# Diffusion steps on Trainium2: who turns the finished sums back into rows

## The chip, the cores and the metric

The kernel runs on one core of one Trainium2 chip. The metric is the device time of one launch in microseconds. The kernel before was run three times: 2592.35, 2608.69 and 2619.11 us, with a median of 2608.69 us.

## The reference, cut to what matters

Four graph layers follow one another on 3125 nodes with 128 features and 50000 edges. Only the last, a diffusion, is touched. With `norm` made of the nodes' degrees (a self loop counts one) and `t_norm` the softmax of `t` over its ten rows, it computes:

```python
def step(h, _):
    h = jax.ops.segment_sum(norm[:, None] * h[row], col, num_segments=N)
    return (h, h)
_, hs = jax.lax.scan(step, x, None, length=STEP - 1)
y = t_norm[0] * x + jnp.einsum('kf,knf->nf', t_norm[1:], hs)
```

Then `y` goes through a weight matrix, bias and ReLU, and is added to the layer's input. All values are 32-bit floats.

## The kernel before, in words

The nine sparse sums are done as dense matrix products. The kernel keeps `counts`, a 3200 by 3200 matrix in 16 bits that says how often each source node sends to each target node. It is cut into 25 blocks of 128 source nodes (`NB`). By Horner's rule a step computes sums over sources of (rows of `y`) times (row of counts) and adds `t_norm[k] * x`; there are nine steps (`STEPS - 1`).

**Matmuls.** In a step each source block `sb` is the stationary operand, 128 nodes by 128 features. So the product comes out turned: features lie on partitions, target nodes on columns. A source is split into a high and a low part in rounded 32-bit form (`U_parts`, `u_part(sb, 0)` and `u_part(sb, 1)`), and both are multiplied and added in PSUM. The last source, 24, has both parts in one block of partitions. Target nodes are cut into four ranges (`RANGES`): three of 896 columns and one of 448. In the first three ranges odd and even columns are separate matmuls of 448 columns. The odd counts are read from `counts` in place as 32-bit words; the even counts have to be converted first into a tile of the ring `T_even` (`TILES` tiles of 448 columns). The fourth range is converted whole. One source in one range is a *piece*: four matmuls in the first three ranges, two in the fourth, half of it for source 24.

**Order.** `visits()` writes the order out. In the middle of a step one source goes through all four ranges (the pieces are `paired`). At a step's ends it is range by range: the first `LAG` sources at the beginning, the last `LAG` at the end. So range 0 is complete before the other ranges, and the next step can begin on its first blocks. Pieces are numbered through all steps, `FULL` = 100 in one step. `range_end` has the place in the step at which each range is complete.

**What goes beside the matmuls.** ScalarE and VectorE each run through all piece numbers n in one loop, and each issues at place n what its tables put there. Both are strictly in order, and a wait holds all that stands behind it.
- Even counts of piece n + `AHEAD`. In paired pieces ScalarE converts ranges 0 and 1 with one instruction (line 2921), VectorE 2 and 3 (line 2997). In unpaired ones they take turns (`by_act`, lines 2924 and 2997). A conversion waits until the piece that used its tile is done.
- `summed(s, r)` (VectorE, lines 2967, 2970 and 2971): once the last piece of a range is done, PSUM plus `t_norm[k]` times the turned input `x` is written to SBUF, in `W[r % 2]`. The turned input has been brought there by a DMA of SyncE's queue from `turned_rows`; for range r the queue waits until the range that last used the same half of `W` has been turned.
- `turn(s, t)` (TensorE, line 2843): up to four blocks of a finished range are transposed against the identity into a PSUM bank. `TURNS` lists seven such groups, with range, first block, blocks and bank; `places` says at which piece numbers they come. In each group TensorE waits for `d_summed`.
- `high(s, t)` (ScalarE, line 2882) and `low(s, t)` (VectorE, line 2956) read the turned blocks from PSUM, scale them by the nodes' degrees and write the high part and the rest as `U_parts` of the next step.

In the last step nothing is turned; `products` multiplies the sums by the weights directly. In the first step sources come in the order `SOURCES`, as their counts return from DRAM, and `turn_h` and `kept` also turn the layer's input for `turned_rows`.

A first matmul of a range in a step waits for `d_summed` (its bank has been read) and, where a bank was also used for turning (`freed`), for `d_split` (its low parts have been made).

Of the kernel before, what the change touches and what calls it, by code (L numbers as in the profile page):

```python
# [13 lines left out]
P = 128  # L14
D = 128
N = 3125
NB = -(-N // P)
# [114 lines left out]
def build(nc, a, out):  # L132
    ctx = ExitStack()
    with ctx:
# [2119 lines left out]
        RANGES = [(0, 2 * HALFW), (2 * HALFW, 2 * HALFW), (4 * HALFW, 2 * HALFW), (6 * HALFW, HALFW)]  # L2254
        TILES = 8
        tiles_at = -(-(tables_at + 32) // P) * P - 32
        turned_at = tiles_at + TILES * HALFW
        U_at = turned_at + 2 * 2 * HALFW
        UW = (NB - 1) * 2 * D + D
# [381 lines left out]

        LAG = 6
        END = NB - LAG

# [11 lines left out]
        def diffusion(begin, ends):  # L2656
# [6 lines left out]
            COUNT = len(PIECE)  # L2663
            AHEAD = 5
            assert COUNT == FULL * (STEPS - 1)
            paired = [len(ranges) == 4 for s, sb, ranges in VISITS for r in ranges]
            by_act = lambda n: PIECE[n][2] < 2 if paired[n] else n % 2 == 0
            evens = [sum(by_act(m) == by_act(n) for m in range(n + 1)) for n in range(COUNT)]
# [5 lines left out]

            TURNS = [(0, 0, 4, 0), (0, 4, 3, 1), (1, 7, 4, 2), (1, 11, 3, 3), (2, 14, 4, 4), (2, 18, 3, 7), (3, 21, 4, 6)]
            NT = len(TURNS)
            places = [range_end[0] + 1, range_end[0] + 3, range_end[1] + 1, range_end[1] + 3, FULL + 1, FULL + 3, FULL + 5]
            turn_at = {FULL * s + place: (s, t) for s in range(STEPS - 2) for t, place in enumerate(places)}
            turns_of = [2, 4, 6, 7]
            freed = {0: 7, 1: 7, 2: 14, 3: 14, 4: 18, 6: NB}  # L2680

            last = STEPS - 2
            GROUPS = [(0, 0, 4, 7), (0, 4, 3, 0), (1, 7, 4, 1), (1, 11, 3, 2), (2, 14, 4, 3), (2, 18, 3, 4), (3, 21, 4, 5)]
            group_at = {FULL * last + place: g for g, place in enumerate((*places[0:4], range_end[2] + 2, range_end[2] + 4))}
            NGS = len(GROUPS)
# [8 lines left out]
            HS = [space.get([2 * P]) for _ in range(3)]  # L2694
            W = [at(turned_at + k * 2 * HALFW, [2 * HALFW]) for k in range(2)]
            space = Space(at, U_at, U_at + END * 2 * D)
            XR = space.get([NB, D])
# [31 lines left out]
            def turned_in(bank, q, n=P):  # L2729
                return banks[0:n, bank, q * P:(q + 1) * P]  # L2730

            def turns_made(s, r):

                return NT * s + turns_of[r]

# [55 lines left out]
            def pe(e):  # L2791
                def matmuls(v):
# [8 lines left out]
                    for j in range(parts):  # L2801
                        weight = U_parts[:, sb * 2 * D + j * D:sb * 2 * D + (j + 1) * D]
                        start, stop = sb == order[0] and j == 0, sb == order[-1] and j == parts - 1
                        for i, r in enumerate(ranges):
                            n = FIRST[v] + i
                            d0, w = RANGES[r]
                            if start and s:
                                e.wait_ge(d_summed, 4 * (s - 1) + r + 1)
                                if 2 * r in freed:
                                    e.wait_ge(d_split, NB * s + freed[2 * r])  # L2810
                            if r < 3:
                                w0 = sb * NP // 2 + d0 // 2
# [18 lines left out]

                def turn(s, t):
                    r, b0, n, bank = TURNS[t]
                    e.wait_ge(d_summed, 4 * s + r + 1)
                    if bank == 7 and s == 0:
                        e.wait_ge(h_copied.sem, h_copied.at(len(PAIRS)))
                    elif bank == 7:
                        e.wait_ge(d_split, NB * s + b0 + n)
                    for q in range(n):
                        b = b0 + q  # L2840
                        c0 = b * P - RANGES[r][0]
                        rows = P if b < LAST else HALF
                        x = e.transpose(turned_in(bank, q, rows), turned_sum(r)[:, c0:c0 + rows], ident)
                    x.then_inc(d_turned, 1)

                def products(g):
# [10 lines left out]
                for v, (s, sb, ranges) in enumerate(VISITS):  # L2857
                    matmuls(v)
                    n = FIRST[v] + len(ranges) - 1
                    if n in pair_at:  # L2860
                        turn_h(pair_at[n])
                    if n in turn_at:
                        turn(*turn_at[n])
                    if n in group_at:
# [3 lines left out]
            def act(e):  # L2868
# [6 lines left out]

                def high(s, t):
                    r, b0, n, bank = TURNS[t]
                    e.wait_ge(d_turned, NT * s + t + 1)
                    for q in range(n):
                        b = b0 + q  # L2880
                        rows = P if b < LAST else HALF
                        e.activation(u_part(b, 0, rows), turned_in(bank, q, rows), ACT.Copy, scale=rows_of(dinv2l, b, rows)[:, b:b + 1]).then_inc(d_hi, 1)

# [27 lines left out]
                for n in range(-8, COUNT):  # L2911
# [16 lines left out]
                    if n in pair_at:  # L2928
                        kept(pair_at[n])
                    if n in turn_at:  # L2930
                        high(*turn_at[n])
                    if n in group_at:
# [7 lines left out]
            def dve(e):  # L2940
# [7 lines left out]

                def low(s, t):
                    r, b0, n, bank = TURNS[t]  # L2950
                    e.wait_ge(d_turned, NT * s + t + 1)
                    e.wait_ge(d_hi, NB * (s + 1) + b0 + n)
                    for q in range(n):
                        b = b0 + q
                        rows = P if b < LAST else HALF
                        e.scalar_tensor_tensor(u_part(b, 1, rows), turned_in(bank, q, rows), rows_of(dinv2l, b, rows)[:, b:b + 1], u_high(b, rows),
                                               ALU.mult, ALU.subtract).then_inc(d_split, 1)
# [31 lines left out]
                for n in range(-8, COUNT):  # L2989
# [569 lines left out]
```

## Time and profile before

| what | before |
|---|---|
| median of 3 runs | 2608.69 us (2592.35 to 2619.11) |
| the profiled execution's own time (its span, first to last instruction) | 2609.8 us |
| TensorE matmul busy | 2312.7 us (89%), 12453 matmuls |
| VectorE busy | 1439.1 us (55%) |
| ScalarE busy | 1231.7 us (47%) |
| GpSimd busy | 1202.3 us (46%) |
| diffusion, first matmul to last sum of the fourth range | 1914.0 to 2598.6 us |

The profile is one execution of the program as the hardware profiler recorded it. The span reaches from its first instruction to its last. Busy times of an engine are sums over its instructions; instructions overlap a little, since the next one starts before the last has ended, so distances between starts say more about throughput than durations do. In the diffusion the matmul records carry modelled ends, and starts are the better guide there too. Times in the order-of-time views are microseconds from the span's start, and what stands in brackets behind a row is how long the engine was idle before it and what it waited for. Tiles are named as `out<-in`: what is written, then what is read.

### The profile page before, as it was taken

The numbers are of one execution on the slowest core, as the hardware profiler recorded it, in microseconds if no ns is written. First come the engines' busy times: TensorE is split into PE (matmuls) and PEld (weight loads), VectorE is DVE, ScalarE is ACT, GpSimd is POOL, SyncE is SP. The second block draws the span as 40 slices with busy tenths as digits, with TensorE's granted clock in tenths as the row PEclk, the third lists the DMA queues.
The fourth block names the chain that finished last, engine by engine and source line by source line (L and its number), as shares of the span: only waits on it lengthen the run. The fifth ranks groups of instructions, "written<-read, shape, count | busy, mean of one in ns | idle before, by whom it ended". The sixth has DMA issues, their size and how long they took to land.

```text
span 2609.8 us, 51354 instructions
## 1 busy us (share of the span) xinstructions
PE 2312.7 (89%) x12453; PEld 1966.3 (75%) x12453; DVE 1439.1 (55%) x6252; ACT 1231.7 (47%) x5343; POOL 1202.3 (46%) x1243
## 2 busy tenths in 40 slices
PE   3778777789539999999989999999989999999998
PEld 2556556555429999999947888888879889988887
DVE  5767777760535665666446777758543433344343
ACT  3656666667313333333233555546454444444443
POOL 3777777720057777777147777777330000000000
PEclk9955555569755555555589989979799999999999
DMA  3242333340334444444054344444452000000002
GB/s 92 60 124 65 123 94 90 122 121 2 91 102 105 108 109 110 110 108 134 21 135 111 105 113 114 113 105 117 139 219 78 29 11 22 18 25 25 25 25 62
DMA packets 174356, 227.43 MB, mean 87 GB/s; under 512 B 63552, under 2 KB 134409, under 8 KB 173929
## 3 DMA queue, kind: packets, MB, share of 16 engines
q0 software_dynamic: 50176, 131.74, 18.9%
q1 hardware_dynamic: 117070, 88.93, 11.2%
q10 hardware_dynamic: 6810, 3.40, 0.5%
q8 instruction: 111, 1.82, 0.3%
q14 instruction: 189, 1.54, 0.2%
HBM read 183.63 MB, written 40.29 MB: 86 GB/s over the span
## 4 chain that ended last, share of the span: by engine, by line
PE 70%; issue 9%; DVE 7%; POOL 5%; ACT 4%; DMA 3%; ACTq 1%; DVEq 0%; SPq 0%; POOLq 0%
PE banks L2817 9%; PE banks L2813 9%; PE banks L1780 6%; PE banks L1781 6%; PE banks L1722 5%; POOL arena L229 4%; PE banks L1783 4%; PE banks L1786 3%; PE banks L755 3%; PE banks L2819 3%; PE banks L967 2%; PE banks L2424 2%; PE banks L1784 2%; PE banks L758 2%; PE banks L782 1%
## 5 line engine op out<-in xcount | busy, mean ns | idle before, releaser
L229 POOL DMA_INDIRECT arena<-value_table,arena x392 | 391.4, 998 | 314.1 <-DMA ed_table<-arena 195.0
L229 POOL DMA_INDIRECT arena<-gat_table,arena x392 | 403.4, 1029 | 198.4 <-issue 86.8
L2813 PE MATMUL banks<-counts,u_parts 128*128 128x448 f32 x1323 | 490.9, 371 | 2.8 <-DVE u_parts L2946 2.8
L2817 PE MATMUL banks<-counts_even,u_parts 128*128 128x448 f32 x1323 | 485.9, 367 | 0.0
L229 POOL DMA_INDIRECT arena<-h_table,arena x392 | 377.5, 963 | 128.1 <-issue 87.8
L2997 DVE CAST counts_even<-counts 128x448 fp32r<-128x448 bf16 x450 | 162.7, 389 | 304.3 <-PE banks L2817 275.4
L755 PE MATMUL banks<-arena 128*128 128x425 bf16 x392 | 208.2, 531 | 112.6 <-ACT arena L811 93.8
L758 PEld LDWEIGHTS banks<-arena 128*128 128x128 f32 x784 | 230.9, 311 | 54.2 <-issue 43.1
L2813 PEld LDWEIGHTS banks<-counts,u_parts 128*128 128x128 f32 x1323 | 249.1, 188 | 23.9 <-ACT arena L2441 3.0
L2817 PEld LDWEIGHTS banks<-counts_even,u_parts 128*128 128x128 f32 x1323 | 249.2, 188 | 21.4 <-ACT counts_even L2921 0.3
L1781 PE MATMUL banks<-arena 128*128 128x17 f32 x784 | 230.6, 375 | 0.0
L1780 PE MATMUL banks<-arena 128*128 128x17 f32 x784 | 228.6, 373 | 0.1
L808 ACT ACTIVATE arena<-banks 128x400 f32 x392 | 207.9, 530 | 36.4 <-DVE banks L744 25.4
L1722 PE MATMUL banks<-arena 128*128 128x512 bf16 (+1 forms) x605 | 216.4, 412 | 3.9 <-DMA ed_table<-arena 3.9
L1871 ACT ACTIVATE arena<-banks 128x32 f32 (+1 forms) x784 | 187.5, 239 | 60.9 <-issue 38.8
L2921 ACT ACTIVATE counts_even<-counts 128x896 fp32r<-128x896 bf16 x123 | 117.4, 954 | 206.0 <-PE banks L2817 194.5
L1781 PEld LDWEIGHTS banks<-arena 128*128 128x128 f32 x784 | 214.2, 333 | 0.0
L1780 PEld LDWEIGHTS banks<-arena 128*128 128x128 f32 x784 | 201.8, 318 | 7.2 <-DVE arena L1653 0.4
L758 PE MATMUL banks<-arena 128*128 128x17 f32 x784 | 176.7, 307 | 12.9 <-DMA arena<-h_table,arena 12.2
L1783 PE MATMUL banks<-arena 128*128 128x136 f32 x784 | 186.3, 323 | 0.0
L1859 ACT ACTIVATE arena<-banks 128x2 f32<-128x2 f32 (+1 forms) x262 | 45.7, 175 | 293.6 <-PE banks L1786 208.0
L755 PEld LDWEIGHTS banks<-arena 128*128 128x128 bf16 x392 | 49.5, 126 | 153.5 <-ACT arena L811 142.3
(298 smaller groups left out, 4842.7 us busy)
## 6 DMA issues: line engine op xcount, KB each, us to landing
adj_rows<-arena SPq DMA_DIRECT2D x5, 4000.0 KB
arena<-ed_table SPq DMA_DIRECT2D x784, 0.5 KB
arena<-turned_rows SPq DMA_DIRECT2D x27, 448.0 KB, 3.3
counts<-adj_rows SPq DMA_DIRECT2D x1, 7200.0 KB, 20.3
arena<-h_table,arena POOLq DMA_INDIRECT x392
arena<-value_table,arena POOLq DMA_INDIRECT x392
arena<-gat_table,arena POOLq DMA_INDIRECT x392
counts<-adj_rows SPq DMA_DIRECT2D x1, 5600.0 KB, 17.6
```

Of the source, the lines that this page charges most:

```text
L229: return e.indirect_dma_start(into, None, table, bass.IndirectOffsetOnAxis(ap=index.bitcast(U32), axis=0))
L755: e.matmul(banks[:, c % RBANK, W1:CS], BY_LO[:, kx, :], BY_HI_D[:, kx, 0:CC], start=True, stop=True, skip_group_check=True)
L758: e.matmul(banks[:, c % RBANK, 0:W1], G[:, k, :], S[:, c // BC % 2, c % BC, :], start=False, stop=True, skip_group_check=True).then_inc(l0 ...
L808: e.activation(first.of(C, j), windows_in(j)[:, 1:, 0:WIN], ACT.Copy, scale=SMALL).then_inc(l0_counted, 1)
L1722: e.matmul(banks[:, 7, 0:n], identb, spare[:, 0:n], start=True, stop=True, skip_group_check=True)
L1780: e.matmul(pv[:, 0, :], rows[:, 0:D], OHF[k3][:, j, :], start=begins, stop=True, skip_group_check=True)
L1781: e.matmul(pv[:, 1, :], rows[:, D + H:], OHV[k3][:, j, :], start=False, stop=True, skip_group_check=True)
L1783: e.matmul(pv[:, 0:H, :], rows[:, 0:D], S[c % RS][:, 0:H, :], start=begins, stop=True, skip_group_check=True)
L1871: e.activation(first.of(acc, c), sums_in(c)[:, :, 0:WIN], ACT.Copy).then_inc(e2_acc, 1)
L2813: e.matmul(banks[:, 2 * r, 0:HALFW], weight, C_odd[:, w0:w0 + HALFW], start=start, stop=stop)
L2817: x = e.matmul(banks[:, 2 * r + 1, 0:HALFW], weight, tile(n), start=start, stop=stop)
L2997: e.tensor_copy(into, counts).then_inc(d_even_dve, 1)
```

## The change

VectorE turns the finished sums, not TensorE. `e.transpose` of VectorE turns 32 by 32 squares. One instruction takes the squares (i, j) of all blocks of a range: it reads partitions 32i to 32i + 31 and writes partitions 32j to 32j + 31 of `V`, a new SBUF region of seven blocks. Sixteen such instructions (`QUADS`) turn a range; in the last range block 24 has 64 nodes, and j of 2 and 3 leave it out. Two instructions are issued at each of eight places in a row. ScalarE's high parts and VectorE's low parts read `V` in SBUF instead of PSUM. `V` holds one range, so `turn` waits until high and low parts of the range before have been made; this follows from the order of the places.

The places are new: counted from one before range 0's end, the sums come at 3, 13, 27 and 33, the turns begin at 5, 19, 34 and 48, the high parts come at 13, 16, 27, 30, 42, 45 and 56, the low parts begin at 15, 29, 44 and 58. `LAG` goes from 6 to 7. The room for `V` comes from the ring of even counts: `TILES` goes from 8 to 6 and `AHEAD` from 5 to 4. In unpaired pieces ScalarE converts two of three, where it was one of two. The matmuls no longer wait for `freed` banks. One addition of weights moves from the third to the fourth step.

```diff
-        TILES = 8
+        TILES = 6
-        U_at = turned_at + 2 * 2 * HALFW
+        U_at = turned_at + 3 * 2 * HALFW
-        LAG = 6
+        LAG = 7
-            AHEAD = 5
+            AHEAD = 4
-            by_act = lambda n: PIECE[n][2] < 2 if paired[n] else n % 2 == 0
+            by_act = lambda n: PIECE[n][2] < 2 if paired[n] else n % 3 > 0
-            TURNS = [(0, 0, 4, 0), (0, 4, 3, 1), (1, 7, 4, 2), (1, 11, 3, 3), (2, 14, 4, 4), (2, 18, 3, 7), (3, 21, 4, 6)]
-            NT = len(TURNS)
-            places = [range_end[0] + 1, range_end[0] + 3, range_end[1] + 1, range_end[1] + 3, FULL + 1, FULL + 3, FULL + 5]
-            turn_at = {FULL * s + place: (s, t) for s in range(STEPS - 2) for t, place in enumerate(places)}
-            turns_of = [2, 4, 6, 7]
-            freed = {0: 7, 1: 7, 2: 14, 3: 14, 4: 18, 6: NB}
+            RANGE_BLOCKS = [(0, 7), (7, 7), (14, 7), (21, 4)]
+            QUADS = [(i, j) for j in range(4) for i in range(4)]
+            NQ = len(QUADS)
+            first_end = range_end[0] - 1
+            at_places = lambda rows: {FULL * s + first_end + p: (s, *v) for s in range(STEPS - 2) for p, v in rows}
+            sum_at = at_places([(3, (0,)), (13, (1,)), (27, (2,)), (33, (3,))])
+            sum_at.update({FULL * (STEPS - 2) + range_end[r] - 1: (STEPS - 2, r) for r in range(4)})
+            turn_at = at_places([(p + k, (r, 2 * k)) for r, p in enumerate((5, 19, 34, 48)) for k in range(NQ // 2)])
+            high_at = at_places([(13, (0, 0, 4)), (16, (0, 4, 3)), (27, (1, 7, 4)), (30, (1, 11, 3)), (42, (2, 14, 4)), (45, (2, 18, 3)), (56, (3, 21, 4))])
+            low_at = at_places([(p + k, (b0 + 2 * k, min(2, n - 2 * k))) for p, (b0, n) in zip((15, 29, 44, 58), RANGE_BLOCKS) for k in range(-(-n // 2))])
+            V = at(turned_at + 2 * 2 * HALFW, [2 * HALFW // P, P])
+            def turned_row(b, rows):
+                return V[0:rows, b - RANGE_BLOCKS[min(b // 7, 3)][0], :]
             def turns_made(s, r):
-                return NT * s + turns_of[r]
+                return NQ * (4 * s + r + 1)
...
                                 e.wait_ge(d_summed, 4 * (s - 1) + r + 1)
-                                if 2 * r in freed:
-                                    e.wait_ge(d_split, NB * s + freed[2 * r])
...
-                def turn(s, t):
-                    r, b0, n, bank = TURNS[t]
-                    e.wait_ge(d_summed, 4 * s + r + 1)
...
-                        x = e.transpose(turned_in(bank, q, rows), turned_sum(r)[:, c0:c0 + rows], ident)
-                    x.then_inc(d_turned, 1)
...
-                def high(s, t):
-                    r, b0, n, bank = TURNS[t]
-                    e.wait_ge(d_turned, NT * s + t + 1)
-                    for q in range(n):
-                        b = b0 + q
+                def high(s, r, b0, n):
+                    e.wait_ge(d_turned, turns_made(s, r))
+                    for b in range(b0, b0 + n):
                         rows = P if b < LAST else HALF
-                        e.activation(u_part(b, 0, rows), turned_in(bank, q, rows), ACT.Copy, scale=rows_of(dinv2l, b, rows)[:, b:b + 1]).then_inc(d_hi, 1)
+                        e.activation(u_part(b, 0, rows), turned_row(b, rows), ACT.Copy, scale=rows_of(dinv2l, b, rows)[:, b:b + 1]).then_inc(d_hi, 1)
...
+                def turn(s, r, q):
+                    b0, n = RANGE_BLOCKS[r]
+                    e.wait_ge(d_summed, 4 * s + r + 1)
+                    if r:
+                        before = NB * (s + 1) + b0
+                    else:
+                        before = NB * (s + 1)
+                    e.wait_ge(d_hi, before)
+                    e.wait_ge(d_split, before)
+                    for i, j in QUADS[q:q + 2]:
+                        blocks_in = n if r < 3 or j < 2 else n - 1
+                        rows = turned_sum(r).rearrange("p (b d) -> p b d", d=P)
+                        e.transpose(V[32 * j:32 * j + 32, 0:blocks_in, 32 * i:32 * i + 32],
+                                    rows[32 * i:32 * i + 32, 0:blocks_in, 32 * j:32 * j + 32]).then_inc(d_turned, 1)
+
+                def low(s, b0, n):
+                    for b in range(b0, b0 + n):
                         rows = P if b < LAST else HALF
+                        e.wait_ge(d_hi, NB * (s + 1) + b + 1)
+                        e.scalar_tensor_tensor(u_part(b, 1, rows), turned_row(b, rows), rows_of(dinv2l, b, rows)[:, b:b + 1], u_high(b, rows),
                                                ALU.mult, ALU.subtract).then_inc(d_split, 1)
...
+                    if n in sum_at:
+                        summed(*sum_at[n])
                     if n in turn_at:
-                        low(*turn_at[n])
-                    if n >= 0 and n % FULL + 1 in range_end:
-                        summed(n // FULL, range_end.index(n % FULL + 1))
-                    if n == FULL * 2:
+                        turn(*turn_at[n])
+                    if n in low_at:
+                        low(*low_at[n])
+                    if n == FULL * 3:
```

## Rows read from the trace of the kernel before

**Rows 1.** The page of the profile: its first line.
```profile
span 2609.8 us, 51354 instructions
```

**Rows 2.** Busy time by stretch: start:end, length, engines, clock, DMA, GB/s; one step.
```profile
2223.00:2298.00 75.00, 74.00 (x371) 66.90 (x371) 29.32 (x84) 32.24 (x62) 0.00 (x0) 1.00 0.08 22
```

**Rows 3.** Instructions of line 2967 alone: ns min/median/max, first and last start.
```profile
L2967 DVE SCALAR_TENSOR_TENSOR arena<-arena,banks x9: 672/679/680, 2000.3 to 2598.6; 128x448 f32<-128x448 f32 x9
```

**Rows 4.** Groups by line, 1850 to 2610: count, busy us, mean ns, idle before.
```profile
L2817 PE MATMUL banks<-counts_even,u_parts 128*128 128x448 f32 x1323 | 485.9, 367 | 0.0
...
L2997 DVE CAST counts_even<-counts 128x448 fp32r<-128x448 bf16 x450 | 162.7, 389 | 304.3 <-PE banks L2817 275.4 <-PE banks L2819 23.6 <-DMA counts<-adj_rows 4.7
...
L2921 ACT ACTIVATE counts_even<-counts 128x896 fp32r<-128x896 bf16 x123 | 117.4, 954 | 206.0 <-PE banks L2817 194.5 <-issue 6.0 <-PE banks L2819 5.5
L2924 ACT ACTIVATE counts_even<-counts 128x448 fp32r<-128x448 bf16 x204 | 114.5, 581 | 86.4 <-PE banks L2817 77.6 <-DMA counts<-adj_rows 4.7 <-PE banks L2819 4.2
...
L2956 DVE SCALAR_TENSOR_TENSOR u_parts<-banks,arena,u_parts 128x128 fp32r<-128x128 f32 (+1 forms) x200 | 57.5, 344 | 61.7 <-ACT u_parts L2882 61.5
L2882 ACT ACTIVATE u_parts<-banks,arena 128x128 fp32r<-128x128 f32 (+1 forms) x200 | 57.5, 366 | 66.4 <-PE banks L2843 66.4
...
L2874 ACT ACTIVATE u_parts<-arena 128x128 fp32r<-128x128 f32 (+1 forms) x25 | 9.5, 406 | 16.0 <-POOL arena L2773 16.0
```

**Rows 5.** Waits from 1900 to 2600: waiter, cause, us in total, times, longest.
```profile
PE banks L2843 <- DVE arena L2971: 4.2, 8, 0.6
...
PE banks L2819 <- DVE counts_even L2997: 4.1, 9, 0.7
```

**Rows 6.** TensorE in order of time at a step's end: start, us, line, count.
```profile
2210.20 0.37 PE L2817 MATMUL banks<-counts_even,u_parts 128*128 128x448 f32 x1
...
2210.77 0.45 PE L2813 MATMUL banks<-counts,u_parts 128*128 128x448 f32 x1
2211.05 0.36 PE L2817 MATMUL banks<-counts_even,u_parts 128*128 128x448 f32 x1
...
2215.45 0.37 PE L2817 MATMUL banks<-counts_even,u_parts 128*128 128x448 f32 x1
2216.39 0.66 PE L2843 MATMUL banks<-arena 128*128 128x128 f32 x4 [0.58 <-DVE arena L2971]
...
2220.06 2.33 PE L2819 MATMUL banks<-counts_even,u_parts 128*128 128x448 f32 x10
2222.82 0.44 PE L2819 MATMUL banks<-counts_even,u_parts 128*128 128x448 f32 x1 [0.44 <-DVE counts_even L2997]
```

**Rows 7.** VectorE in order of time, the same step's end and the next step.
```profile
2208.97 0.68 DVE L2970 SCALAR_TENSOR_TENSOR arena<-arena,banks 128x448 f32<-128x448 f32 x1 [2.47 <-PE banks L2817]
...
2210.16 0.38 DVE L2997 CAST counts_even<-counts 128x448 fp32r<-128x448 bf16 x1
...
2226.64 1.13 DVE L2956 SCALAR_TENSOR_TENSOR u_parts<-banks,arena,u_parts 128x128 fp32r<-128x128 f32 x4 [2.36 <-ACT u_parts L2882]
...
2230.64 1.25 DVE L2956 SCALAR_TENSOR_TENSOR u_parts<-banks,arena,u_parts 128x128 fp32r<-128x128 f32 x4 [1.13 <-ACT u_parts L2882]
2231.91 1.30 DVE L2997 CAST counts_even<-counts 128x448 fp32r<-128x448 bf16 x4
...
2244.30 0.69 DVE L2997 CAST counts_even<-counts 128x448 fp32r<-128x448 bf16 x2 [2.26 <-PE banks L2817]
...
2272.97 0.69 DVE L2997 CAST counts_even<-counts 128x448 fp32r<-128x448 bf16 x2 [2.17 <-PE banks L2817]
```

**Rows 8.** VectorE group of line 3006, shapes apart, 1950 to 2550.
```profile
L3006 DVE TENSOR_TENSOR arena<-arena 128x128 f32<-128x128 f32 x1 | 0.3, 285 | 0.0
```

**Rows 9.** ScalarE in order of time at the same step's end.
```profile
2211.05 1.14 ACT L2882 ACTIVATE u_parts<-banks,arena 128x128 fp32r<-128x128 f32 x4 [1.91 <-PE banks L2843]
...
2213.77 1.05 ACT L2924 ACTIVATE counts_even<-counts 128x448 fp32r<-128x448 bf16 x2
```

**Rows 10.** DMA issues by line: KB each, median us to landing.
```profile
arena<-turned_rows SPq DMA_DIRECT2D x27, 448.0 KB, 3.3
```

More of the change, by code:

```diff
@@ L2673, in diffusion @@
             pair_at = {4 * (j + 4) + 3: j for j in range(len(PAIRS))}
-            TURNS = [(0, 0, 4, 0), (0, 4, 3, 1), (1, 7, 4, 2), (1, 11, 3, 3), (2, 14, 4, 4), (2, 18, 3, 7), (3, 21, 4, 6)]
-            NT = len(TURNS)
-            places = [range_end[0] + 1, range_end[0] + 3, range_end[1] + 1, range_end[1] + 3, FULL + 1, FULL + 3, FULL + 5]
-            turn_at = {FULL * s + place: (s, t) for s in range(STEPS - 2) for t, place in enumerate(places)}
-            turns_of = [2, 4, 6, 7]
-            freed = {0: 7, 1: 7, 2: 14, 3: 14, 4: 18, 6: NB}
+            RANGE_BLOCKS = [(0, 7), (7, 7), (14, 7), (21, 4)]
[8 more added lines that the diff above has]
+            low_at = at_places([(p + k, (b0 + 2 * k, min(2, n - 2 * k))) for p, (b0, n) in zip((15, 29, 44, 58), RANGE_BLOCKS) for k in range(-(-n // 2))])
+            places = [range_end[0] + 1, range_end[0] + 3, range_end[1] + 1, range_end[1] + 3]
             last = STEPS - 2
             GROUPS = [(0, 0, 4, 7), (0, 4, 3, 0), (1, 7, 4, 1), (1, 11, 3, 2), (2, 14, 4, 3), (2, 18, 3, 4), (3, 21, 4, 5)]
-            group_at = {FULL * last + place: g for g, place in enumerate((*places[0:4], range_end[2] + 2, range_end[2] + 4))}
+            group_at = {FULL * last + place: g for g, place in enumerate((*places, range_end[2] + 2, range_end[2] + 4))}
             NGS = len(GROUPS)
@@ L2830, in turn_h @@
                     x.then_inc(h_turned.sem, 1)
-                def turn(s, t):
-                    r, b0, n, bank = TURNS[t]
-                    e.wait_ge(d_summed, 4 * s + r + 1)
[L2835 to L2838, printed above, removed]
-                    for q in range(n):
-                        b = b0 + q
-                        c0 = b * P - RANGES[r][0]
-                        rows = P if b < LAST else HALF
-                        x = e.transpose(turned_in(bank, q, rows), turned_sum(r)[:, c0:c0 + rows], ident)
-                    x.then_inc(d_turned, 1)
                 def products(g):
@@ L2861, in pe @@
                         turn_h(pair_at[n])
-                    if n in turn_at:
-                        turn(*turn_at[n])
                     if n in group_at:
@@ L2874, in high_first @@
                     e.activation(u_part(sb, 0), rows_of(TX[n % 3], sb), ACT.Copy, scale=rows_of(dinvl, sb)[:, sb:sb + 1]).then_inc(d_hi, 1)
-                def high(s, t):
-                    r, b0, n, bank = TURNS[t]
-                    e.wait_ge(d_turned, NT * s + t + 1)
-                    for q in range(n):
-                        b = b0 + q
+                def high(s, r, b0, n):
+                    e.wait_ge(d_turned, turns_made(s, r))
+                    for b in range(b0, b0 + n):
                         rows = P if b < LAST else HALF
-                        e.activation(u_part(b, 0, rows), turned_in(bank, q, rows), ACT.Copy, scale=rows_of(dinv2l, b, rows)[:, b:b + 1]).then_inc(d_hi, 1)
+                        e.activation(u_part(b, 0, rows), turned_row(b, rows), ACT.Copy, scale=rows_of(dinv2l, b, rows)[:, b:b + 1]).then_inc(d_hi, 1)
                 def kept(j):
@@ L2929, in act @@
                         kept(pair_at[n])
-                    if n in turn_at:
-                        high(*turn_at[n])
+                    if n in high_at:
+                        high(*high_at[n])
                     if n in group_at:
@@ L2947, in low_first @@
                                            ALU.mult, ALU.subtract).then_inc(d_split, 1)
[L2949 to L2954, printed above, removed]
+                def turn(s, r, q):
[14 more added lines that the diff above has]
+                    for b in range(b0, b0 + n):
                         rows = P if b < LAST else HALF
-                        e.scalar_tensor_tensor(u_part(b, 1, rows), turned_in(bank, q, rows), rows_of(dinv2l, b, rows)[:, b:b + 1], u_high(b, rows),
+                        e.wait_ge(d_hi, NB * (s + 1) + b + 1)
+                        e.scalar_tensor_tensor(u_part(b, 1, rows), turned_row(b, rows), rows_of(dinv2l, b, rows)[:, b:b + 1], u_high(b, rows),
                                                ALU.mult, ALU.subtract).then_inc(d_split, 1)
```

## The prediction, made before the changed kernel was run

> **What bounds the kernel now.** The page gives the span [rows 1]; the three runs of the kernel before took 2592.35 to 2619.11 us with a median of 2608.69, so the profiled span lies 1.1 us above the median, and I make the sum against the span. The change touches only the nine diffusion steps. First I read the busy times of one step: TensorE is busy 74.00 of 75 us, VectorE 29.3, ScalarE 32.2, and the granted clock is 1.00, its 2.4 GHz level [rows 2]. TensorE sets the time there; the other two have room on average. Then the length of a step: the ninth sum of the last range starts 598.3 us after the first [rows 3], so a step takes 74.8 us. Then the pure matmul time: in the middle of a step one source (14 matmuls of 448 columns) takes (2272.97 - 2244.30)/10 = 2.867 us [rows 7], 0.205 us a matmul. A step has 24 sources of 14 and one of 7 matmuls, 343 in all, 70.3 us. The excess is **4.5 us a step**, and no change that leaves the matmuls alone can win more than 8 x 4.5 = 36 us.
>
> The order of time shows where the excess is. A group of four turns puts 0.57 us between its neighbours where 0.205 would do, and 0.075 more behind the next matmul: 0.44 us; a group of three by proportion 0.33 [rows 6]. A step has four groups of four and three of three: 2.75 us. The first turn group of the second range waits for its sum: it starts 0.74 us late. At the end of the fourth range a matmul starts at 2222.82 where ten after 2220.06 would give 2222.11: 0.71 us late, for even counts that VectorE had not yet converted [rows 6]. Both recur in nearly every step [rows 5]. Together 4.2 of the 4.5 us.
>
> **The change, part by part.** I count pieces (a source times a range) within a step from 0 to 99, 100 being the first of the next step. A piece of the first three ranges is 0.82 us, of the fourth 0.41, of source 24 half of that.
>
> *Removed from TensorE:* 200 turns and their waits, the 4.5 us above, if nothing else is late.
>
> *Added to VectorE:* 64 square instructions a step, 48 of seven blocks (224 elements a partition) and 16 of four or three. No row shows such an instruction, so I bound it. An SBUF instruction of 128 elements lasts 285 ns [rows 8]; the slope from 344 ns at 128 elements to 679 at 448 is 1.05 ns an element [rows 3, 4], so 224 elements last 385 ns, or 444 from the 344 ns row. Instructions of like placement start before the last has ended: four of line 2956 take 1.13 us, 0.26 apart. But where the fourth writes from partition 64 on, the four take 1.25 us: it starts 0.12 us later, about 0.03 after the end of the one before [rows 7]. Each square reads from another group of 32 partitions than the one before, so I let none overlap: 385 + 35 = 420 ns to 480 ns. I take **0.43 us**, near the low end because a square, like the instruction of [rows 8], has no PSUM operand. Outer bounds: 0.30 (the casts move 448 elements at a pitch of 0.30 [rows 7]) and 0.71 (each element counted twice: the 679 ns row and 35).
>
> By the Trainium skill, "VectorE: DVE Perf Modes", section "Two Vector instructions with no wait between them", an instruction is held until all earlier ones finish when its start quadrant differs from the last one's; the 1.25 against 1.13 us agrees. The section "The three transpose paths" of the same page gives 311 ns for a VectorE transpose of 128 by 128 in bf16; an estimate from it is 311 + 100 + 35 = 446 ns a square, by which the sum below would come out at the time before.
>
> *The other edits.* Even counts at a step's ends go to ScalarE in two of three cases; ScalarE needs 0.47 us each when back to back (1.05 - 0.58) [rows 4, 9], VectorE 0.30. The ring of six tiles, converted four ahead, leaves a piece at least four piece times of lead. In the middle of a step the tightest cast is the third range's: its tile is free after the ninth matmul of the source before (1.84 us), it is wanted at the sixth of its own (2.87 + 1.03 = 3.9) and lasts 0.39: covered, nothing, and if that cover went each 0.1 us of lateness would cost 0.1 in each of 11 sources. Seven sources at the ends give 28 pieces in which the next step needs only the first range: that is what the late squares live on. The rows' DMA for the fourth range now waits for the second range's squares; it lands 3.3 us later [rows 10], at 23.4 us on the clock below against a sum at 23.7, so it is covered by a hair. High parts read SBUF, 406 against 366 ns [rows 4].
>
> *The ledger of one boundary*, clock at 0 when piece 80 starts. TensorE without stalls starts piece 100 at 12.5, 121 at 29.7, 124 at 30.9 and 128 at 32.6 us. VectorE starts the first sum at -0.3. Until the third range is turned (place 119) it has three sums of 1.19 and one of 0.6, 13 casts of 0.30, 14 low parts of 0.26 and 48 squares: 11.7 + 48 x 0.43 = 32.3, with 0.3 of small waits it ends at **32.4**. The first range's low parts are due at 12.5 and done at about 11; the casts stay less than four pieces behind until place 105. So the first two ranges cost nothing, or some tenths. But ScalarE stands at place 120 in its high parts, waiting for those squares, and the casts of 125 to 127 and the double cast of 128 are queued behind. After 32.4 it needs 1.3 for four high parts (1.14 [rows 9] and their longer reads), 0.94 for two casts, 0.87 for three high parts and 0.95 for the double cast [rows 4]: 36.5. TensorE wants those even counts at 32.8. **Stall 3.7 us.** What VectorE then does (seven low parts, the last 16 squares at about 0.32) lags less than this stall and the four-ahead lead.
>
> Net 4.5 - 3.7 = 0.8 us a step, 6 us in eight: 2609.8 - 6 = 2603.4, less the 1.1 about **2602 us**. Each 0.01 us of a square moves this by 0.48 x 8 = 3.8 us; break-even is 0.447 us.
>
> **The rivals.**
> *Squares cheap.* If they overlap or stream faster, the stall falls, but not to nothing: ScalarE cannot begin place 120 before piece 118 ends at 28.9, and 0.5 + 1.3 + 0.94 + 0.87 + 0.95 after it is 33.5, a stall of 0.7. Reached at 0.37 us and below. Gain 8 x 3.8 = 30 us: 2579 profiled, 2578. For it: 0.26 us pitches abound [rows 7]. Against: the held fourth instruction.
> *Squares dear, slower.* At 0.48 to 0.50 us (the 344 ns row, with a semaphore step in each) VectorE ends the third range at 34.8 to 35.8, and ScalarE's queue at place 120 stalls TensorE 6.1 to 7.1 us: 1.6 to 2.6 a step lost, 2622 to 2630. It decides from 0.447 us. For it: only 15 to 50 ns more than I took. Against: the 285 ns of [rows 8].
> *Squares at half rate*, 0.60 to 0.71 us: stall 12 to 17 us, 60 to 100 us lost, 2668 to 2709. Against: nothing in the rows says that a 4-byte element counts twice.
>
> **How the numbers follow.** Forecast (0.40 to 0.46 us a square, 2590 to 2613): 0.47. Cheap: 0.23. Dear: 0.21. Half rate: 0.07, the rest 0.02. Slower by over 1% (above 2635, about the least a measurement of this kernel can tell from no change) takes the half rate and the upper tail of dear, 0.13; faster by over 1% (below 2582.6) needs at most 0.38 us, 0.21; within 1% 0.66. The range is 2576 to 2640: cheap, forecast and dear, with the half rate and a little of both tails left out.
>
> **What would show it.** A median square of seven blocks of 395 ns starting about 0.43 us after the last; no TensorE wait for line 2971; ScalarE's waits for TensorE's turns replaced by waits for the squares, longest at the third range; TensorE's idle before the fourth range's pieces 125 to 127 and the first double cast, 3 to 4 us a boundary; steps of about 74.0 us. It is wrong if a square's pitch is under 0.38 or over 0.48 us, if ScalarE's high parts find their squares done, or if the stall sits in the first 28 pieces on casts of VectorE.

## The result and the profile after

| | before | changed |
|---|---|---|
| median of 5 runs | 2608.69 us (2592.35 to 2619.11) | 2630.02 us (2619.74 to 2634.35) |
| ratio, 95% interval | | 1.0089 (1.0059 to 1.0119) |
| profiled span | 2609.8 us | 2629.4 us (its own time 2631.2) |
| diffusion: first to last matmul of odd counts | 679.3 us | 703.4 us |
| ... first matmul to first sum of range 0 | 72.9 us | 81.4 us |
| ... a step, from its range-0 sum to the next, mean of 8 | 74.4 us | 76.1 us |
| ... last range-0 sum to last matmul of odd counts | 11.5 us | 13.1 us |

The change made the kernel 0.9% slower. The diffusion alone grew by 24.1 us: 8.5 before its first sum, 8 x 1.75 = 14.0 in the steps, 1.6 at the end. Part of the first and the last term is only moved. With seven sources at the end, range 0 is complete three pieces earlier (one source in ranges 1, 2 and 3: ten matmuls, 2.0 us), and eight more matmuls of odd counts come behind the last range-0 sum. These eight are the whole 1.6 us at the end, and on equal work the first part grew by 10.5 us. (The rest of the kernel, which the change leaves alone, was 4.5 us shorter in this execution.)

The groups of the diffusion by line, in the changed kernel; the columns are those of [rows 4], and lines 2825, 2827, 2999, 2911, 2914, 2958 and 2872 are 2817, 2819, 2997, 2921, 2924, 2956 and 2882 of before (line 2827 has the matmuls of the fourth range, line 2951 the squares):

```profile
L2825 PE MATMUL banks<-counts_even,u_parts 128*128 128x448 f32 x1323 | 491.8, 372 | 11.9 <-DVE counts_even L2999 5.0 <-ACT counts_even L2911 4.0 <-ACT counts_even L2914 2.8
L2951 DVE STREAM_TRANSPOSE arena<-arena 32x224 f32<-32x224 f32 (+2 forms) x512 | 191.1, 373 | 15.7
L2914 ACT ACTIVATE counts_even<-counts 128x448 fp32r<-128x448 bf16 x318 | 170.7, 571 | 110.5 <-PE banks L2825 102.5 <-DMA counts<-adj_rows 4.4 <-PE banks L2827 3.7
L2999 DVE CAST counts_even<-counts 128x448 fp32r<-128x448 bf16 x370 | 145.0, 394 | 206.8 <-PE banks L2825 194.5 <-DMA counts<-adj_rows 5.0 <-PE banks L2827 2.5
...
L2827 PE MATMUL banks<-counts_even,u_parts 128*128 128x448 f32 x441 | 138.2, 379 | 27.8 <-DVE counts_even L2999 11.5 <-ACT counts_even L2914 9.1 <-ACT u_parts L2872 3.3
...
L2872 ACT ACTIVATE u_parts<-arena 128x128 fp32r<-128x128 f32 (+1 forms) x200 | 64.4, 390 | 83.8 <-DVE arena L2951 83.8
```

TensorE's two stalls of before, for line 2971 and for one late cast [rows 5, 6], have been replaced by stalls on every supplier of even counts. ScalarE's high parts now wait 83.8 us for the squares. The squares of seven blocks alone:

```profile
L2951 DVE STREAM_TRANSPOSE arena<-arena 32x224 f32<-32x224 f32 x384 | 154.5, 402 | 12.0
```

One boundary on VectorE, in order of time (start, us; the prediction's clock zero is 2220.33; rows of before: [rows 7]):

```profile
2220.03 0.68 DVE L2972 SCALAR_TENSOR_TENSOR arena<-arena,banks 128x448 f32<-128x448 f32 x1
...
2222.18 0.39 DVE L2999 CAST counts_even<-counts 128x448 fp32r<-128x448 bf16 x1 [0.88 <-PE banks L2825]
2222.49 2.55 DVE L2951 STREAM_TRANSPOSE arena<-arena 32x224 f32<-32x224 f32 x6
2225.07 0.40 DVE L2999 CAST counts_even<-counts 128x448 fp32r<-128x448 bf16 x1
2225.50 2.57 DVE L2951 STREAM_TRANSPOSE arena<-arena 32x224 f32<-32x224 f32 x6
...
2253.95 0.84 DVE L2951 STREAM_TRANSPOSE arena<-arena 32x224 f32<-32x224 f32 x2
```

Six squares take 2.57 us, so the pitch is (2.57 - 0.402)/5 = 0.434 us. The last square of the third range ends at 2254.79, which is 34.5 us on the clock where 32.4 was predicted. ScalarE at the same boundary, first at the high parts of the second range, then at those of the third:

```profile
2242.36 1.28 ACT L2872 ACTIVATE u_parts<-arena 128x128 fp32r<-128x128 f32 x4 [4.53 <-DVE arena L2951]
...
2254.83 1.28 ACT L2872 ACTIVATE u_parts<-arena 128x128 fp32r<-128x128 f32 x4 [2.64 <-DVE arena L2951]
2256.01 1.03 ACT L2914 ACTIVATE counts_even<-counts 128x448 fp32r<-128x448 bf16 x2
2256.94 0.97 ACT L2872 ACTIVATE u_parts<-arena 128x128 fp32r<-128x128 f32 x3
2257.82 1.78 ACT L2911 ACTIVATE counts_even<-counts 128x896 fp32r<-128x896 bf16 x2
```

And every idle stretch of TensorE at this boundary, with the eight matmuls before the longest:

```profile
2232.00 1.80 PE L2827 MATMUL banks<-counts_even,u_parts 128*128 128x448 f32 x7 [0.44 <-DVE counts_even L2999]
2238.46 0.47 PE L2825 MATMUL banks<-counts_even,u_parts 128*128 128x448 f32 x1 [0.23 <-DVE counts_even L2999]
2241.50 0.47 PE L2825 MATMUL banks<-counts_even,u_parts 128*128 128x448 f32 x1 [0.33 <-DVE counts_even L2999]
2244.16 0.47 PE L2825 MATMUL banks<-counts_even,u_parts 128*128 128x448 f32 x1 [0.76 <-ACT counts_even L2914]
2253.05 2.07 PE L2827 MATMUL banks<-counts_even,u_parts 128*128 128x448 f32 x8
2256.71 1.47 PE L2827 MATMUL banks<-counts_even,u_parts 128*128 128x448 f32 x6 [1.60 <-ACT counts_even L2914]
2258.81 0.47 PE L2825 MATMUL banks<-counts_even,u_parts 128*128 128x448 f32 x1 [0.41 <-ACT counts_even L2911]
```

The brackets sum to 3.8 us; the starts tell more. Against 0.205 us a matmul these places and the matmuls behind them are 6.1 us late in all (2253.05 plus eight matmuls is 2254.69, and the next starts at 2256.71). The last queue is as the prediction drew it: squares, four high parts, two casts, three high parts, double cast, TensorE. It starts 2.1 us later. But it holds only 3.1 of the 6.1 us. The other 3.0 us are lost before it, at the first four brackets: at the end of the fourth range and in the first two ranges of the next step, three times for a cast of VectorE that comes late behind or between its squares, and once (2244.16) for a cast of ScalarE that stood behind its 4.53 us wait for the second range's squares. The clock has no part in this: the granted clock from 2000 to 2300 us is 1.00 before and 0.99 in the changed kernel.

### The profile page after: what moved, and what is told of

The parts are those of the page before. It is cut to its first block, busy times and chain, and to the rows that moved or that the text cites. A ratio compares the mean times of both kernels' runs of the same rounds, so it can differ in the third digit from the quotient of the medians.

```text
span 2629.4 us, 51690 instructions
## 1 busy us (share of the span) xinstructions
PE 2298.6 (87%) x12253; PEld 1934.8 (74%) x12253; DVE 1609.5 (61%) x6684; ACT 1276.7 (49%) x5440; POOL 1205.9 (46%) x1243
## 4 chain that ended last, share of the span: by engine, by line
PE 62%; issue 12%; DVE 11%; POOL 5%; ACT 5%; DMA 3%; ACTq 1%; DVEq 0%; SPq 0%; POOLq 0%
PE banks L2825 7%; PE banks L2821 7%; PE banks L1780 6%; PE banks L1781 6%; PE banks L1722 5%; POOL arena L229 5%; PE banks L1783 4%; DVE arena L2951 3%; PE banks L1786 3%; PE banks L755 3%; PE banks L967 2%; PE banks L2424 2%; PE banks L2827 2%; PE banks L1784 2%; PE banks L758 2%
## 5 line engine op out<-in xcount | busy, mean ns | idle before, releaser
L229 POOL DMA_INDIRECT arena<-value_table,arena x392 | 397.2, 1013 | 312.7 <-DMA ed_table<-arena 193.6
L2825 PE MATMUL banks<-counts_even,u_parts 128*128 128x448 f32 x1323 | 491.8, 372 | 11.9 <-DVE counts_even L2999 5.0
L2825 PEld LDWEIGHTS banks<-counts_even,u_parts 128*128 128x128 f32 x1323 | 250.3, 189 | 46.7 <-DVE counts_even L2999 11.5
L2999 DVE CAST counts_even<-counts 128x448 fp32r<-128x448 bf16 x370 | 145.0, 394 | 206.8 <-PE banks L2825 194.5
L2914 ACT ACTIVATE counts_even<-counts 128x448 fp32r<-128x448 bf16 x318 | 170.7, 571 | 110.5 <-PE banks L2825 102.5
L2951 DVE STREAM_TRANSPOSE arena<-arena 32x224 f32<-32x224 f32 (+2 forms) x512 | 191.1, 373 | 15.7
```

The costliest lines, as they stand in the source:

```text
L229: return e.indirect_dma_start(into, None, table, bass.IndirectOffsetOnAxis(ap=index.bitcast(U32), axis=0))
L2951: e.transpose(V[32 * j:32 * j + 32, 0:blocks_in, 32 * i:32 * i + 32], rows[32 * i:32 * i + 32, 0:blocks_in, 32 * j:32 * j + 32]).then_inc( ...
```

## The experiments

Each ran against the kernel before on the same chip; the changed kernel itself was not run again beside them, so "faster than the changed kernel" is read from the two ratios. "Step" is the mean distance of range-0 sums, "first" the time from the first matmul of the diffusion to its first sum, both of the profiled execution. They tell the parts apart more sharply than the whole time does, which scatters by up to 1% from run to run (2592 to 2619 us for the kernel before).

| kernel | ratio to before, 95% interval | first, us | step, us |
|---|---|---|---|
| before | 1 | 72.9 | 74.4 |
| changed | 1.0089 (1.0059 to 1.0119) | 81.4 | 76.1 |
| b_ring: before, small ring | 1.0041 (1.0001 to 1.0081) | 81.4 | 74.4 |
| b_lag: before, seven sources | 0.9961 (0.9939 to 0.9983) | 73.4 | 72.8 |
| b_rest: before, all but the squares | 0.9977 (0.9947 to 1.0008) | 80.9 | 72.9 |
| a_small: changed, squares of one block | 0.9886 (0.9819 to 0.9953) | 81.5 | 70.1 |
| a_late: changed, third range later | 1.0002 (0.9969 to 1.0035) | 81.2 | 73.5 |
| a_half: changed, casts one to one | 1.0138 (1.0066 to 1.0211) | 82.5 | 77.7 |
| a_ahead3: changed, three ahead | 1.0093 (1.0062 to 1.0125) | 85.9 | 76.3 |
| a_lowodd: changed, low parts one later | 1.0056 (1.0030 to 1.0081) | 71.6 | 76.2 |
| a_spread: changed, squares spread | 0.9934 (0.9905 to 0.9963) | 80.9 | 71.4 |
| a_spread_lowodd: both | 0.9927 (0.9897 to 0.9957) | 71.7 | 71.4 |

**b_ring**

```diff
-        TILES = 8
+        TILES = 6
-            AHEAD = 5
+            AHEAD = 4
```

> The kernel before, with one part of the change alone: six tiles of even counts and four ahead instead of eight and five (TensorE still turns). In its loops VectorE then waits at place n for piece n - 2 instead of n - 3. Theory A (the smaller ring costs in the first step, where VectorE's low parts, GpSimd and TensorE's turns of the input form one cycle; the rest of the loss comes from the squares): first step 5 to 10 us longer, later steps at most 0.5 us longer than 74.8, in all 6 to 14 us slower than before. Theory B (the smaller ring is the whole loss, in the step boundaries too): about 20 us slower, later steps near 76.4 us. Theory C (the ring is harmless, as the prediction had it): no difference, first step as before.

The first part is 8.4 us longer and the later steps are unchanged (74.4). Theories B and C fall. The changed kernel's first part is as long with ten matmuls (2.0 us) less in it; about as much comes back with seven sources (b_lag below).

**a_small**

```diff
-                        blocks_in = n if r < 3 or j < 2 else n - 1
+                        blocks_in = 1
```

> The changed kernel with every square instruction cut to one block (32 elements a partition instead of 224, 128 or 96); six of seven blocks are not turned, all instructions and waits stay. A square should last about 0.20 us and start 0.23 us after the last. Theory A (VectorE's squares set the end of each boundary): 48 x 0.2 = 9.6 us less VectorE work before the third range is turned, TensorE's excess at a boundary falls from 6.1 to 1 or 2 us, steps of 71.2 to 72.2 us, 32 to 40 us faster than the changed kernel, so about 12 to 20 us faster than before; the first step stays as long as in the changed kernel. Theory B (ring): time stays near 2630 us, steps near 76.4.

```profile
L2951 DVE STREAM_TRANSPOSE arena<-arena 32x32 f32<-32x32 f32 x512 | 103.7, 203 | 15.8
```

A square lasts 203 ns, 0.20 less than the 402 of seven blocks, and the step falls by 6.0 us to 70.1, which is the pure matmul time of 70.2 us, lower than expected. So with 48 x 0.2 = 9.6 us less of squares nothing is left of the boundary's stall: ring and ScalarE's larger share cost nothing there by themselves, as b_rest below shows too. The first part is unmoved.

**a_late**

```diff
-            turn_at = at_places([... enumerate((5, 19, 34, 48)) ...])
+            turn_at = at_places([... enumerate((5, 19, 34, 58)) ...])
-            high_at: (42, (2, 14, 4)), (45, (2, 18, 3)), (56, (3, 21, 4))
+            high_at: (52, (2, 14, 4)), (54, (2, 18, 3)), (66, (3, 21, 4))
-            low_at: zip((15, 29, 44, 58), RANGE_BLOCKS)
+            low_at: zip((15, 29, 54, 68), RANGE_BLOCKS)
```

> The changed kernel with the third range's high parts moved from places 42 and 45 to 52 and 54 (behind the casts of the fourth range's last pieces and the first double cast), its low parts to 54 to 57, the fourth range's squares to 58 to 65, high parts 66, low parts 68 and 69. Theory A (ScalarE's wait for the third range's squares holds up the casts queued behind it): the stall of 2.0 us in the fourth range's pieces and the 0.6 us before the first double cast go; the 3.1 us of VectorE's late casts in the first two ranges stay; steps of 73.7 to 74.7 us, 14 to 22 us faster than the changed kernel, about equal to before. Rival (VectorE alone is the bound, so the stall only moves to its own casts of the paired pieces): steps stay within 0.7 us of 76.4.

The step falls by 2.6 us to 73.5, just below the expected range, and of TensorE's idle stretches at the same boundary only the first four are left (here the first and the last of them):

```profile
2231.46 1.79 PE L2827 MATMUL banks<-counts_even,u_parts 128*128 128x448 f32 x7 [0.44 <-DVE counts_even L2999]
...
2243.61 0.47 PE L2825 MATMUL banks<-counts_even,u_parts 128*128 128x448 f32 x1 [0.76 <-ACT counts_even L2914]
```

So the last link of the predicted queue, ScalarE standing at place 120 with casts behind it, is shown: it costs 2.6 us a step, 3.1 at the boundary above. What stays there is the 3.0 us lost before it.

**a_ahead3**

```diff
-            AHEAD = 4
+            AHEAD = 3
```

> The changed kernel with even counts converted three pieces ahead instead of four, so that at place n a conversion waits for piece n - 3, as in the kernel before, with the ring of six. Theory A (in the first step the link to the piece, not the number of tiles, lengthens the cycle): the six waits of 1.6 us of the fourth range's matmuls in the first step shrink to the 0.7 us waits of before, 4 to 8 us there; at the boundaries the lead is a piece shorter but TensorE is bound to the end of the squares anyway, steps within 0.5 us of 76.4. Rival (the shorter lead costs a piece time at each stall): steps 0.8 us or more longer, 6 us or more slower in all.

Theory A was wrong on the first part: it grew by 4.5 us instead of shrinking. On the later steps it was right (76.3). The distance between a cast and the piece it waits for is not the cause. The order of time showed another (VectorE of the changed kernel in the first step, then TensorE):

```profile
1947.55 0.35 DVE L2936 SCALAR_TENSOR_TENSOR u_parts<-arena,u_parts 128x128 fp32r<-128x128 f32 x1 [3.12 <-ACT u_parts L2866]
1947.82 0.39 DVE L2999 CAST counts_even<-counts 128x448 fp32r<-128x448 bf16 x1
```

```profile
1943.08 0.47 PE L2827 MATMUL banks<-counts_even,u_parts 128*128 128x448 f32 x1 [1.62 <-DVE counts_even L2999]
...
1948.26 0.47 PE L2827 MATMUL banks<-counts_even,u_parts 128*128 128x448 f32 x1 [1.62 <-DVE counts_even L2999]
```

The cast that TensorE waits for stands behind a low part of the first step, and that waits 3.12 us for ScalarE's high part, this for GpSimd's product, this for TensorE's turn of the input: a cycle of 5.18 us a source where the kernel before has 4.25. b_ring has the same cycle, 5.19 us with six waits of 1.62. With five ahead the fourth range's cast is issued one place earlier, ahead of the low part; with three ahead the third range's cast falls behind it too.

**a_lowodd** takes that order back without touching the ring:

```diff
-                    if n % 2 == 0 and (n + 8) // 2 < NB:
-                        low_first((n + 8) // 2)
+                    if n % 2 and (n + 7) // 2 < NB:
+                        low_first((n + 7) // 2)
```

> The changed kernel with VectorE's low parts of the first step at odd places, one later, so that the fourth range's cast stands ahead of the low part that waits for ScalarE and GpSimd. Theory D (with four ahead instead of five this cast falls behind that low part in VectorE's queue, and TensorE waits 1.6 us for it six times): first matmul to first sum of the diffusion 81.4 us now, then 74 to 77; later steps unchanged at 76.1; 4 to 8 us faster than the changed kernel. Rival (six tiles are too few for that step, wherever the low part stands): 81 us as now.

The first part falls by 9.8 us to 71.6, more than expected, with six tiles still. TensorE's waits of the fourth range's matmuls for VectorE's casts, in the list of line 2827 over the whole diffusion, changed kernel and then this one:

```profile
  DVE counts_even L2999: 28.0, 25
```

```profile
  DVE counts_even L2999: 4.2, 9
```

By the starts of the matmuls, the stretch with the cycle (matmuls 60 to 166) is 8.6 us over its pure time before, 14.9 in b_ring and in the changed kernel and 5.4 here. So the order of two instructions explains 6.3 of the 8.4 us of b_ring, and turned round it wins more than the ring lost. The other 2.2 us of b_ring lie among the first 60 matmuls; b_lag, whose ring is the old one, has 1.3 us there too, so how much of them belongs to the ring stays open.

**a_half**

```diff
-            by_act = lambda n: PIECE[n][2] < 2 if paired[n] else n % 3 > 0
+            by_act = lambda n: PIECE[n][2] < 2 if paired[n] else n % 2 == 0
```

> The changed kernel with the even counts of unpaired pieces shared one to one again (n % 2), not two to one. VectorE has 20 instead of 13 casts until the third range is turned, each 0.43 us when it stands between squares. Theory A (VectorE's own list of work sets the end of each boundary): 7 x 0.43 = 3 us more a step, steps of 78.5 to 79.5 us, 20 to 28 us slower than the changed kernel. Rival (ScalarE's share of casts and its double cast is what TensorE waits for): steps of 74.5 to 75.5 us.

Slower, as theory A says, but by 1.6 us a step, not 3. (Only the steps show it: the ratio's interval overlaps the changed kernel's.) ScalarE has as many casts less, and its queue behind the squares is shorter; I take this for the other half, but no run shows it apart.

**b_rest** and **b_lag** are the kernel before with parts of the change:

```diff
-        LAG = 6
+        LAG = 7
-        TILES = 8
+        TILES = 6
-            AHEAD = 5
+            AHEAD = 4
-            by_act = lambda n: PIECE[n][2] < 2 if paired[n] else n % 2 == 0
+            by_act = lambda n: PIECE[n][2] < 2 if paired[n] else n % 3 > 0
```

> The kernel before with every part of the change but the squares: seven sources at a step's ends, six tiles and four ahead, two of three unpaired casts by ScalarE; TensorE still turns. If the squares are what costs at the boundaries, later steps stay at 74.4 us within 0.5 (sums of the first range to the next), and only the first step is long: first matmul to first sum 80 to 82 us though that sum now comes three pieces (2.5 us) earlier; in all 8 to 12 us slower than before. Rival (seven sources or ScalarE's larger share cost at the boundaries too): steps of 75 us or more.

b_lag has the first of the four edits alone.

> The kernel before with seven sources at a step's ends instead of six, and nothing else. If seven sources cost nothing in themselves: steps of 74.4 us within 0.3, first matmul to first sum 70.4 us (72.9 less three pieces), last first-range sum to last matmul 14 us instead of 11.5, time as before. Rival (the order of the first step's last sources makes TensorE wait for the counts that return last): 1 to 3 us more in the first step.

Both expectations missed on the steps: seven sources do not leave the step as it was. They win 1.6 us in b_lag and 1.5 in b_rest, where the squares are absent in both, and b_rest is not 8 to 12 us slower than before but within the noise of it. They remove the two stalls that stand beside TensorE's turns [rows 5, 6]: in b_lag no turn waits for a sum any more, and the turns' own 2.5 us a step are all of the excess that is left.

In the first part b_lag has 2.6 us more than ten matmuls less would give. Half of it is what the rival said, a wait for the counts that return last (1.3 us by the starts; 1.5 to 1.8 in the other kernels with seven sources). The order of time of b_lag:

```profile
1979.60 0.44 PE L2813 MATMUL banks<-counts,u_parts 128*128 128x448 f32 x1 [0.89 <-DMA counts<-adj_rows]
```

The other 1.3 us lie among the first 34 matmuls of the diffusion, which the edit does not touch; their cause stays open.

**a_spread** and **a_spread_lowodd** keep every instruction and move the squares:

```diff
-            sum_at: ..., (33, (3,))
+            sum_at: ..., (37, (3,))
-            turn_at = at_places([(p + k, (r, 2 * k)) for r, p in enumerate((5, 19, 34, 48)) for k in range(NQ // 2)])
+            turn_at = at_places([(p + w * k // 2, (r, 2 * k)) for r, (p, w) in enumerate(((5, 2), (19, 3), (50, 4), (72, 4))) for k in range(NQ // 2)])
-            high_at: (27, ..), (30, ..), (42, ..), (45, ..), (56, ..);  low_at: (15, 29, 44, 58)
+            high_at: (31, ..), (34, ..), (66, ..), (68, ..), (88, ..);  low_at: (15, 33, 68, 90)
```

> The changed kernel with its squares spread: the second range's over places 19 to 29, the fourth sum at 37, the third range's squares at every second place from 50 to 64, the fourth's from 72 to 86, high and low parts behind each. No work less. Theory A (VectorE's work until place 119, 34.8 us, exceeds TensorE's 29.3 there, while VectorE waits 2.06 us of every 2.87 in the paired pieces that follow): steps of 70.8 to 72.3 us, 30 to 40 us faster than the changed kernel, 10 to 20 faster than before. Rival (squares in paired pieces delay the casts there as much as they did at the boundary): steps of 75 us or more.

> Both: the spread squares and the low parts of the first step at odd places. If the two costs are separate, their gains add: first matmul to first sum 74 to 77 us and steps of 70.8 to 72.3 us, 35 to 48 us faster than the changed kernel, 15 to 28 us faster than before. Rival (one hides the other): no more than the spreading alone.

The step falls from 76.1 to 71.4 us with the same 512 squares of the same 373 ns mean:

```profile
L2951 DVE STREAM_TRANSPOSE arena<-arena 32x224 f32<-32x224 f32 (+2 forms) x512 | 191.2, 373 | 15.8
...
L2872 ACT ACTIVATE u_parts<-arena 128x128 fp32r<-128x128 f32 (+1 forms) x200 | 63.5, 389 | 34.6 <-DVE arena L2951 34.3
```

The two remedies add up in the profile (first 71.7, step 71.4, diffusion 656.0 us against 679.3 of before). Both together ran at a median of 2585.84 us, 2604.79 for the kernel before on that chip: 0.73% faster than before. It has the lowest ratio here of the versions that do all the work, but the intervals of a_spread and of b_lag, the kernel before with one number changed, overlap its own. Only the profiles tell them apart (diffusion 665.3 and 669.1 us); no run sets it beside b_lag on one chip.

## Why the prediction was wrong

The sign was wrong: 6 us faster was forecast, 21 us slower measured. That the time lay in the stated range says little for the mechanism: 8.5 us of the loss come from the first part of the diffusion, which the sum did not look at.

- **What the turns cost on TensorE: a little too high.** The excess of 4.5 us a step was averaged to the last step's fourth sum, and the last step is longer. From range-0 sum to range-0 sum it is 74.37 - 70.24 = 4.13 us. This is 0.4 us a step or 3 us of the miss.
- **A square, right.** 402 ns against 395 assumed, a pitch of 0.434 against 0.43. That none overlaps was read off one late instruction of line 2956 [rows 7], and it held for all. By the Trainium skill, "VectorE: DVE Perf Modes", section "Two Vector instructions with no wait between them", a change of start quadrant holds an instruction, and the trace agrees both ways: behind a cast the first square, which reads and writes from partition 0, starts after 0.31 us (2222.18 to 2222.49), the seventh, at 2225.50, which starts at other partitions, after 0.43.
- **The ledger of one boundary, the step that failed.** It gave the right list and the right last queue, but an end of 32.4 us where 34.5 was measured, and a stall of 3.7 where 6.1 was (5.9 in the mean). The squares were costed as held, the casts between them were not: eight of the 13 casts until place 119 take 0.43 us to the next instruction instead of 0.30, 1.0 us. The cast at place 83 waits 0.88 us for piece 81, whose tile it needs; the ledger had 0.3 us for all waits. The rest, about 0.5 us, is squares and low parts each a few ns longer than taken and the gaps at changes of shape. The 2.1 us by which VectorE is late come back as 2.4 more of stall on TensorE. "So the first two ranges cost nothing, or some tenths" failed too: 3.0 of the 6.1 us are lost there and at the end of the fourth range just before, behind the squares of the first two ranges. By the ledger's own chain they don't add to the total, which the end of the third range's squares sets; but they are what a_late keeps when ScalarE's last queue is taken out (2.6 us a step won, not 5.9). a_small shows that without the time of the squares no stall is left.
- **"The other edits: nothing", wrong in the first step.** The middle of a later step was reckoned, and there it is right (b_ring: 74.4). The first step, where low parts of the input stand in the same queue, was not looked at. It lost 8.4 us (b_ring), 6.3 of them by an order of two instructions (a_lowodd, 9.8 us won).
- **Seven sources** were counted as room for the squares, not as a gain of their own or a cost in the first part (1.3 us of waiting for counts in b_lag). They are worth 1.6 us a step without the change (b_lag). Measured from there the squares cost 76.1 - 72.9 = 3.2 us a step: 6.0 lost on VectorE (a_small: 76.1 - 70.1), 72.9 - 70.1 = 2.8 won on TensorE, the 2.75 us of the prediction.
- **The rivals.** "Squares dear" named the right queue, and its stall of 6.1 to 7.1 us is about what was measured, but the dearness lay in the casts between the squares. That its 2622 to 2630 us holds the measured time is partly luck: 8.5 us of the loss are in the first part, which this rival has not, and 4.5 us came back in the rest of the kernel. "Squares cheap" and "half rate" are excluded by the 402 ns row. The first 28 pieces do show stalls on VectorE's casts, which the prediction listed as a sign that it is wrong.

In numbers: 6.4 us faster in the sum; 8 x (4.5 - 4.13) = 3.0 for the excess, 8 x (5.88 - 3.7) = 17.4 for the stall (5.88 is the mean, 76.12 - 70.24), 8.5 and 1.6 for the first and the last part make it 24.1 us slower for the diffusion, as was measured.

## What to carry to other kernels

Work that is moved to an engine with a low average load lands in that engine's queue at one place; add up the queue between two deadlines, with the neighbours of the new instructions at their new pitch too, before the average is believed. When a ring or a lead is shortened by one, go through every place where the same loop issues something else that waits: the order of two instructions in the first step cost 6.3 us, nearly half of the 14.0 that all later boundaries lost. And undo each part of a change by itself: one part of this one (seven sources) made the kernel before 0.4% faster when it stood alone.

## What the runs showed that was not expected

- The step falls to 70.1 us with small squares: with half of the squares' time out of VectorE, TensorE runs the 343 matmuls of a step back to back at a pitch of 0.204 to 0.205 us, with all waits still in the program. Waits that are met in time cost nothing measurable here.
- A cast of 448 elements over all 128 partitions lasts 389 ns in the mean before and 394 in the changed kernel, but the next instruction starts 0.30 us after it in a row of casts and 0.43 us after it between squares of 32 partitions.
